# A windowed attention on one Trainium2 core: how the token products are formed, which engine normalises, and when statistics are taken

## The reference, cut to what matters

```python
disp = (x @ w_disp + b_disp).reshape(Bx, Tx, NH, BD).transpose(0, 2, 1, 3)
val = (x @ w_val + b_val).reshape(Bx, Tx, NH, HS).transpose(0, 2, 1, 3)
disp_win = _windows(disp, delta)                       # 32 tokens back
strain = disp_win - disp[:, :, :, None, :]
strain_for_state = strain @ w_state + b_state
state = (strain_for_state * cmask_f[None, None, :, :, None]).sum(axis=3) / valid_counts[None, None, :, None]
state_win = _windows(state, delta)
bond_act = gelu(strain @ w_strain + b_strain + state[:, :, :, None, :] @ w_state_i + state_win @ w_state_j + rel_emb @ w_pos)
bond_logits = (bond_act @ w_bond_out)[..., 0] + b_bond_out[0]
damage_act = gelu(strain @ w_damage + b_damage)
damage = jax.nn.sigmoid((damage_act @ w_damage_out)[..., 0] + b_damage_out[0])
logits = bond_logits - damage * 10.0
weights = jax.nn.softmax(jnp.where(cmask[None, None], logits, -jnp.inf), axis=-1)
out = jnp.einsum('bntd,bntde->bnte', weights, val_win)
```

## Time and profile before

| | us |
|---|---|
| median of 3 runs | 3185.65 |
| lowest and highest | 3184.71 and 3186.94 |
| the profiled execution | 3191.0 |
| its span, first to last instruction | 3189.3 |

### The profile page before, as it was taken

How to read it: one execution, slowest core, us unless ns; L and a number is a source line. 1 busy time by engine, 2 the same in 40 slices (tenths; PEclk the granted TensorE clock), 3 DMA queues, 4 the chain that set the end, 5 groups by cost and what they waited for, 6 DMA issues and landing times. The chain is left out here.

```text
span 3189.3 us, 54032 instructions
## 1 busy us (share of the span) xinstructions
PE 2881.4 (90%) x19465; PEld 2047.0 (64%) x19465; DVE 1665.2 (52%) x4524; ACT 1528.2 (48%) x2579; POOL 1339.6 (42%) x1331
## 2 busy tenths in 40 slices
PE   4899999767899999668999997999879999988999
PEld 4799999722344333257999996666546666655666
DVE  4411111168888888554111111566676666655666
ACT  1133333247988888611333332333247777772333
POOL 3544444358999999435444443000043444320000
PEclk9899999978999999868999998999989999999999
DMA  8199999800544444861999997100052333301000
GB/s 281 41 299 327 324 321 327 243 14 14 63 60 59 60 60 60 81 209 41 302 326 323 327 325 240 29 0 0 15 139 71 75 94 98 85 2 37 13 13 20
DMA packets 359983, 431.82 MB, mean 135 GB/s; under 512 B 86449, under 2 KB 314694, under 8 KB 356678
## 3 DMA queue, kind: packets, MB, share of 16 engines
q1 hardware_dynamic: 335174, 395.17, 44.5%
q0 software_dynamic: 24576, 33.57, 5.0%
HBM read 355.80 MB, written 72.88 MB: 134 GB/s over the span
## 5 line engine op out<-in xcount | busy, mean ns | idle before, releaser
L1675 ACT ACTIVATE f_h_t<-f_h_ps,f_b_t 128x128 f32<-128x128 f32 x1024 | 319.4, 363 | 601.2 <-PE f_h_ps L1633 596.2
L2069 POOL TENSOR_TENSOR a_dmg_buf<-a_c 128x2048 f32<-128x2048 f32 x128 | 520.1, 4090 | 63.8 <-PE a_dmg_ps L2117 34.0
L1633 PEld LDWEIGHTS f_h_ps<-f_rows_t,f_w 128*128 128x128 f32 x4096 | 482.7, 194 | 9.9 <-issue 3.5
L1633 PE MATMUL f_h_ps<-f_rows_t,f_w 128*128 128x128 f32 x4096 | 483.9, 277 | 2.3 <-DVE f_rows_t L1687 1.2
L1647 PE MATMUL f_y_ps<-f_w,f_h_t 128*128 128x256 f32 x2048 | 483.5, 379 | 0.0
L1593 POOL DMA_INDIRECT acc_rows<-f_y,f_give x128 | 205.0, 1602 | 491.5 <-DMA acc_rows<-f_y,f_give 460.3
L1647 PEld LDWEIGHTS f_y_ps<-f_w,f_h_t 128*128 128x128 f32 x2048 | 369.9, 190 | 39.9
L1687 DVE COPY f_rows_t<-f_t_ps 128x256 f32<-128x256 f32 x128 | 54.3, 425 | 602.3 <-PE f_t_ps L1621 597.6
L2434 DVE SCALAR_TENSOR_TENSOR a_bond_buf<-a_a,a_small_rep,a_q_ps 128x512 f32<-128x512 f32 x512 | 346.6, 740 | 7.4 <-PE a_q_ps L2234 5.1
L428 DVE SCALAR_TENSOR_TENSOR x_resid<-f_y_ps,f_gate,x_resid 128x256 f32 x512 | 218.9, 479 | 163.6 <-PE f_y_ps L311 158.0
L885 ACT ACTIVATE a_prob<-a_prob,a_neg_top 128x384 f32<-128x384 f32 (+3 forms) x512 | 276.6, 570 | 47.1 <-POOL a_neg_top L702 46.9
(11 more groups left out here) (353 smaller groups left out, 4174.6 us busy)
## 6 DMA issues: line engine op xcount, KB each, us to landing
f_w<-in_L_ffn_w_dram SPq DMA_DIRECT2D x256, 1024.0 KB
a_skewed<-skew SPq DMA_DIRECT2D x32, 512.0 KB, 6.8
a_k_s<-parts SPq DMA_DIRECT2D x16, 768.0 KB, 7.9
acc_rows<-x_resid SPq DMA_DIRECT2D x17, 512.0 KB, 5.3
xn_rows<-f_xn SPq DMA_DIRECT2D x16, 512.0 KB, 3.0
x_resid<-acc_rows SPq DMA_DIRECT2D x16, 512.0 KB, 7.4
a_vals<-val_rows SPq DMA_DIRECT2D x64, 128.0 KB, 3.8
skew<-a_bond SPq DMA_DIRECT2D x128, 64.0 KB, 10.2
```

Of the source, the lines that this page charges most:

```text
L1633: last = nc.tensor.matmul(h_ps[n // HB][:, (n % HB) * P:(n % HB + 1) * P], w1_sb[s][:, c, n * P:(n + 1) * P], rows_t[e % 2][:, c, :], star ...
L1675: nc.scalar.activation(h_t[k][:, n, :], h_ps[n // HB][:, (n % HB) * P:(n % HB + 1) * P], ACT.Gelu, bias=b1_t[:, n, e:e + 1]).then_inc(gelu ...
L2069: nc.gpsimd.tensor_tensor(dmg_buf[n % RING][:, :, :], places(c_sb[h], first_place(dg)), c_sb[h][:, PAD:].unsqueeze(1).broadcast_to([P, DG, ...
```

## The change

1. disp itself is made (DISP, two passes: xn transposed times w_disp, with b_disp added by VectorE's copy), then transposed (DT, two passes), and the means are those of disp. a, c and q are products of `disp_t` and the means with the five block-diagonal 128 x 128 matrices of `inner`: two products each for a and q, one for c. `token_w` and its making at the entry go away. The bank has NTP = 12 passes a batch; the steps of all passes are set anew, and the first values pair is in step 3 instead of 7.
2. ScalarE normalises (Identity with scale 1/std and bias −mean/std, two instructions each in steps 2 and 3) instead of GpSimd. VectorE makes `less_mean` = −mean/std.
3. In the softmax, GpSimd's subtraction goes from step 3 to 4 (after one more damage chunk), the exponentials from 5 to 6 and the sums from 7 to 8; after the last batch they keep their old places.
4. The statistics of batches 1 to 7, their square root and the split of the output bias are at the entry, between the passes of batch 0.

The core of the diff (lines that are only "..." mark what is left out):

```diff
-    NTP = 8
-    XN, XM, A0, C0, A1, C1 = 0, 2, 4, 5, 6, 7
-    A1_Q, C1_Q, Q1_Q = 0, 3, 4
-    V_Q = (7, 15)
-    XN_Q, XM_Q, A0_Q, C0_Q, Q0_Q = 6, 8, 10, 12, 13
+    NTP = 12
+    XN, DISP, DT, XM, A0, C0, A1, C1 = 0, 2, 4, 6, 8, 9, 10, 11
+
+    A1_Q, C1_Q, Q1_Q = 0, 1, 2
+    V_Q = (3, 15)
+    XN_Q, DISP_Q, DT_Q, XM_Q, A0_Q, C0_Q, Q0_Q = 4, 6, 8, 10, 12, 13, 14
+
+    NORM_Q = 2
+
+    TOP_Q, LESS_Q, EXP_Q, SUM_Q = 3, 4, 6, 8
...
         def softmax_batch(s, q):
+
             i, now = divmod(s, STEPS)
+            if i == B and q > TOP_Q:
+                q -= 1
             return i - 1 if now == q and 0 < i <= B else None
...
-            load(b_disp_sb[:, :], b_disp.rearrange("(h p) -> p h", p=P), allow_slow_non_contiguous=True)
+            load(b_disp_r[:, :], b_disp.partition_broadcast(P))
...
-                if q == 4 and i + 1 < B:
-                    normalise(i + 1)
...
+            def make_disp(i, pair):
+                pe.wait_ge(tok_copied, i * NTP + DISP + pair)
+                if i == 0 and pair == 0:
+                    pe.wait_ge(disp_loaded, 16)
+                for j in range(2):
+                    at = PAD + (2 * pair + j) * P
+                    for c in range(DC):
+                        last = nc.tensor.matmul(tok_ps[:, j * D:(j + 1) * D], xn_t[i % NX][:, c, at:at + P],
+                                                w_disp_sb[:, c, :], start=c == 0, stop=c == DC - 1)
+                last.then_inc(tok_ready, 1)
+
+            def turn_disp(i, h):
+                pe.wait_ge(tok_copied, i * NTP + DT + h)
                 for j in range(TPB):
...
+                    last = nc.tensor.transpose(tok_ps[:, j * P:(j + 1) * P], disp[:, j, h * P:(h + 1) * P], core.ident[:, :])
+                last.then_inc(tok_ready, 1)
...
+            def make_q(i, h):
                 if i:
                     pe.wait_ge(bond_pre, (i - 1) * STEPS + (h + 1) * NQ)
...
+                pe.wait_ge(tok_copied, i * NTP + XM + HALF)
+                nc.tensor.matmul(q_ps[h][:, :], flat(inner[:, TO_Q, :, :]), disp_t[:, h, :], start=True, stop=False)
+                nc.tensor.matmul(q_ps[h][:, :], flat(inner[:, TO_Q_MEAN, :, :]), xm_t[:, h, :],
+                                 start=False, stop=True).then_inc(q_ready, 1)
...
+            def normalise(i, tiles):
+                act.wait_ge(rstd_ready, min(i, 1) + 1)
+                if i:
+                    act.wait_ge(tok_ready, (i - 1) * NTP + XN + DC)
+                for j in tiles:
+                    n = i * TPB + j
+                    last = nc.scalar.activation(xn[:, j, :], core.tile(i + 1, j), ACT.Identity,
+                                                bias=less_mean[:, n:n + 1], scale=rstd[:, n:n + 1])
+                if TPB - 1 in tiles:
+                    last.then_inc(xn_ready, 1)
...
-                if s == 3:
-                    act.wait_ge(var_ready, 2)
-                    nc.scalar.activation(std[:, TPB:], std[:, TPB:], ACT.Sqrt).then_inc(std_ready, 1)
...
+                if q in (NORM_Q, NORM_Q + 1) and i + 1 < B:
+                    normalise(i + 1, (2 * (q - NORM_Q), 2 * (q - NORM_Q) + 1))
...
             def inverse_std(first, end, count):
                 dve.wait_ge(std_ready, count)
...
+                nc.vector.reciprocal(rstd[:, tiles], std[:, tiles])
+                nc.vector.drain()
+                nc.vector.scalar_tensor_tensor(out=less_mean[:, tiles], in0=mean_var[:, tiles, 0], scalar=-1.0,
+                                               in1=rstd[:, tiles], op0=ALU.mult, op1=ALU.mult).then_inc(rstd_ready, 1)
...
+            bn_stats(1, 3)
+            copy_disp(0, 0)
+            bn_stats(3, 4)
+            copy_disp(0, 1)
...
             for h in range(HALF):
...
+                copy_disp_t(0, h)
+            split_bias()
+            copy_means(0, 0)
+            bn_stats(4, 5)
+            copy_means(0, 1)
...
             nc.vector.drain().then_inc(biases_ready, 1)
+            bn_stats(5, B)
+            aggregate(1, B)
             copy_a(0, 0)
+            variances(1, B)
             copy_c(0, 0)
+            inverse_std(1, B, 2)
             dve.wait_ge(pads_ready, 1)
             bond_chunk(0)
```

More of the change, by code:

```diff
@@ L2093, in _ @@
                     damage_chunk(s + 1)
[L2094 removed]
+                j = softmax_batch(s, LESS_Q)
                 if j is not None:
                     less_top(j)
[L2097 to L2098 removed]
         @block.tensor
@@ new lines, in turn_disp, with turn_means @@
+            def turn_disp(i, h):
+                pe.wait_ge(tok_copied, i * NTP + DT + h)
+                for j in range(TPB):
+                    last = nc.tensor.transpose(tok_ps[:, j * P:(j + 1) * P], disp[:, j, h * P:(h + 1) * P], core.ident[:, :])
+                last.then_inc(tok_ready, 1)
+            def turn_means(i, h):
+                pe.wait_ge(tok_copied, i * NTP + XM + h)
+                for j in range(TPB):
+                    last = nc.tensor.matmul(tok_ps[:, j * P:(j + 1) * P], disp[:, j, h * P:(h + 1) * P],
@@ L2238, in begin_a @@
-            def begin_a(i, h):
-                pe.wait_ge(tok_copied, i * NTP + (A0, A1)[h])
-                for c in range(DC):
-                    nc.tensor.matmul(tok_ps[:, :], token_w[:, c, h, TO_A, :], xn_t[i % NX][:, c, PAD:],
-                                     start=c == 0, stop=False)
-            def end_a(i, h):
-                for c in range(DC):
-                    last = nc.tensor.matmul(tok_ps[:, :], token_w[:, c, h, TO_A_MEAN, :], xm_t[:, c, :],
-                                            start=False, stop=c == DC - 1)
-                last.then_inc(tok_ready, 1)
+                pe.wait_ge(tok_copied, i * NTP + XM + HALF)
@@ L2291, in _ @@
+                nc.tensor.matmul(tok_ps[:, :], flat(inner[:, TO_C, :, :]), disp_t[:, h, :],
+                                 start=True, stop=True).then_inc(tok_ready, 1)
             pe.wait_ge(small_ready, 1)
@@ L2564, in bn_stats, with aggregate @@
                         nc.vector.bn_stats(stats[:, i * TPB + j, :], core.tile(i + 1, j))
-            def variances(first, end):
+            def aggregate(first, end):
                 nc.vector.drain()
@@ L2569, in variances @@
                     nc.vector.bn_aggr(mean_var[:, t, :], stats[:, t, :])
+            def variances(first, end):
                 nc.vector.drain()
@@ L2575, in inverse_std @@
                 dve.wait_ge(std_ready, count)
-                nc.vector.reciprocal(rstd[:, first * TPB:end * TPB], std[:, first * TPB:end * TPB]).then_inc(rstd_ready, 1)
+                tiles = slice(first * TPB, end * TPB)
+                nc.vector.reciprocal(rstd[:, tiles], std[:, tiles])
+                nc.vector.drain()
+                nc.vector.scalar_tensor_tensor(out=less_mean[:, tiles], in0=mean_var[:, tiles, 0], scalar=-1.0,
+                                               in1=rstd[:, tiles], op0=ALU.mult, op1=ALU.mult).then_inc(rstd_ready, 1)
             bn_stats(0, 1)
+            aggregate(0, 1)
             variances(0, 1)
             nc.vector.tensor_copy(select[:, :, :], core.ident[0:BD, 0:BD].unsqueeze(1).broadcast_to([BD, HH, BD]))
-            dve.wait_ge(std_ready, 1)
-            nc.vector.reciprocal(rstd[:, 0:TPB], std[:, 0:TPB])
-            nc.vector.drain()
-            for j in range(TPB):
-                last = nc.vector.tensor_scalar(xn[:, j, :], core.tile(1, j), mean_var[:, j, 0:1], rstd[:, j:j + 1],
-                                               ALU.subtract, ALU.mult)
-            last.then_inc(xn_ready, 1)
+            inverse_std(0, 1, 1)
             dve.wait_ge(rel_loaded, REL_LOADED)
```

247 lines of the change are left out of this document (94 added, 153 removed).

## The result

The changed kernel takes 3168.28 us (median of 6 runs, 3150.57 to 3171.87), the kernel before beside it 3186.3 (6 runs, 3184.71 to 3188.63): a ratio of 0.9936, 95% interval 0.9922 to 0.9951. It is 18 us faster where 43.9 had been forecast. A second thing stands in these numbers: the runs of the changed kernel lie 21 us apart here, those of the kernel before 4. (When both were run again, the two spreads were 20 and 22 us, so the difference did not repeat.)

What follows compares the result with a forecast made beforehand. The limit was taken to change by quarter: TensorE in first and last, nobody in the second, GpSimd in the third. Gains 16.5 + 1.7 + 22 + 3.7 = 43.9 off 3185.65 gave 3141.8 us, range 3120 to 3172.

Steps and rivals of the forecast that it cites:

- batch 0: First batch of the phase: two ScalarE waits, 5.56 and 12.85 us, close; 64.6 us instead of 87.65, 23.0 less.
- entry, first GELU later by: Before the loop: added statistics and split cost 2.7 us, `less_mean` waiting for GpSimd's chunk 3.8; first GELU 6.5 later.
- batch 1: Second batch: pays 2.0 us for ScalarE's normalising, saves waits of 2.81 and 0.88; gains 1.7.
- five steady batches: Batches 2 to 6: each falls to 75.9 us, a gain of 4.4; 22 together.
- batch 7: Last batch: no normalising to pay for, saves the 2.81 and 0.88 us waits whole; gains 3.7.
- rival D: Identity isn't in the GELU table: four loads of 1.28 us in each of seven batches, 36 us; 3178 us; chance 3%.
- The second quarter: Second four steps of a steady batch: ScalarE's 21.0 us busy stays, waits of 2.81 and 0.88 go; 21.0 instead of 24.75.
- VectorE's in the third: Third four steps of a steady batch: VectorE's 18.5 us of work less a lead won earlier gives 17.9 instead of 18.69.
- rival C: Twelve passes chain through bank `tok_ps`, each waiting for VectorE's copy: a batch 8.7 us slower, 3230; decides from 6.8; chance 8%.
- the entry's paragraph: Entry account, closing that after this reciprocal no VectorE instruction of the loop reads SBUF alone; batch 0 with entry 16.5 us less.
- The step that failed: Softmax weights' stores: exponentials one step later cost nothing, since they have until step 13, seven steps later.
- rival A: Only the holes close: steady batch stays at 80.3 us, only 16.5 of batch 0 and 3.7 of batch 7 remain; 3165; chance 18%.

Runs made afterwards that it cites:

- the other two edits: Changed kernel with weights loaded between the stores and `less_mean` ahead of c's copy, here together with the earlier row sums: 3134.94 us, again 3137.61, ratio 0.9825 both times.
- the second trace: The changed kernel run again without edit, on another chip: median 3176.1 us, ratio 0.9918; its profiled execution 3175.3.
- the entry alone: Kernel before with only the statistics of batches 1 to 7, their square root and the output bias split moved to the entry: 3183.16 us, ratio 0.9953.

## Why the prediction was right and wrong

By its own terms, against the profiled execution of after:

| term | forecast | measured |
| --- | --- | --- |
| batch 0 | 23.0 | 23.4 |
| entry, first GELU later by | 6.5 | 8.2 |
| batch 1 | 1.7 | 1.6 |
| five steady batches | 22 | 14.9 |
| batch 7 | 3.7 | 3.8 |
| phase | 43.9 | 35.3 |
| the median of the runs | 43.9 | 18 |

**Right.** The holes of batch 0 closed to 64.29 us (64.6 forecast), without a wait of ScalarE. Identity needed no table load between GELUs, as the rows of step 2 show, so rival D is out; the four activations advance ScalarE by 2 × (4.77 − 3.79) = 1.96 us (2.0). The rule of the Trainium skill, page "ScalarE: Activation LUTs", section "Table sets: the hidden batching unit", that identity is in every set, agrees with these rows. The estimate of 585 ns by section "What ACT_TABLE_LOAD costs" of the same page of the Trainium skill agrees with the 589 ns of the group. The second quarter is 20.86 (21.0). `less_mean` took 4.38 us (3.8 of waiting forecast), until 679.63, where GpSimd's first chunk ends at 679.59 in the trace, and 0.19 when it came ahead of that chunk. By the rule of the Trainium skill, page "SBUF — State Buffer", section "Who interferes with whom", a VectorE instruction with two SBUF inputs contends with a GpSimd instruction that reads SBUF; the trace agrees, and the experiment that moved it shows that it could be avoided. Batch 1's 1.6 us (1.7 forecast) are in part luck: its second quarter won 3.1 and its third 0.9, and the fourth lost 0.5, with the wait for the weights in it.

**Sizes.** The entry came 8.2 us later instead of 6.5, inside its bounds. Of the steady batch's 4.4 us, 3.0 came: in batch 4 the first two quarters are 18.65 and 20.86 as forecast, the third is 18.62 instead of 17.9, the fourth stayed at 19.13 instead of 18.2. The term that failed is VectorE's in the third: I took the row sums as work that its lead would absorb (18.5 less a lead). VectorE is busy for only 14.61 of the 18.62, so its amount of work sets nothing; it is the place of the row sums in the order that counts, behind a wait of 3.06 us for TensorE. With them ahead of it, and the other two edits, the five steady batches average 75.4 and 76.0; that 75.9 had been forecast is in part luck, since it is the third quarter that fell below its forecast (16.2 to 17.4 for 17.9) while the fourth stayed above (18.4 to 20.7 for 18.2). In that fourth quarter TensorE is busy for 18.51 us and waits most of the rest for a copy of the means. So rival C, the chain through the one token bank, is real in part: TensorE waits for copies out of it for 5.0 to 6.6 us a steady batch (up to 7.0 in the second trace, 0.5 to 1.2 before), about the 6.8 from which it would decide. But 2.2 us of that lie in the second quarter, which ScalarE fills, and cost nothing; in batch 4 the 2.36 and 0.95 us of the last two quarters are what is left. One reading of the entry's paragraph was wrong, without an effect on the sum: VectorE does read SBUF alone in the loop, in the row sums and their reciprocal.

**The step that failed.** "The exponentials one step later cost their stores nothing: they have until step 13, seven steps later." I counted steps and didn't price the way: sixteen stores issued in 17 to 23 us in the two traces of after, then four loads which land after a median of 7.2 and 8.8. Where TensorE waited for them in the loop of these traces, the weights came 28.1 to 34.8 us after the exponentials' end; in batch 1, where nothing else holds the loop, TensorE wants them after 26.6 (the run with the loads between the stores, in which it doesn't wait). In the kernel before it had 31.1 us and more. Every gain between step 6 and step 13 shortens that time further, so my other terms worked against this one. Between the two traces of after the waits alone differ by 11 us in the loop and 2 in the tail, and the phase by 21, nearly all of it in the batches with such a wait and in the tail. Not all of that is the wait's: 1.9 us are in step 11 of batch 2, ahead of it. The account closes roughly: the terms above are 8.6 us short of the forecast, and the loads between the stores gave back 0.4 to 0.6%, 12 to 18 us, of the other 17. The median happens to lie at the 3165 of rival A, but not for its reason: the steady batch did not stay at 80.3.

The sign, the range and most terms held; the likeliest value was wrong by the transfer that was put at nothing, and by a smaller part in the steady batch. How often that transfer is waited for can't be said from two traces of the changed kernel; both have such a wait.

**Open.** In many batches of every variant step 11 or 12 lasts 1 to 4 us longer than in others of the same run. VectorE's division starts late, in part of them put down to a releaser that the trace names only as remote. From the run with the loads between the stores, batch 6:

```profile
1187.26 0.42 DVE L2476 TENSOR_TENSOR a_ctx<-a_o_ps,a_inv_sum 128x256 f32<-128x256 f32 x1 [3.30 <-remote]
```

TensorE's sums for it had ended at 1185.01 by their modelled ends. In another part it is TensorE that stands idle without a named releaser: in batch 2 of nine of the eleven traces with the new token products it stops behind the fourth of the same eight products, at the same instruction each time, for 1.0 to 4.2 us (the row of 4.18 above). In each of the nine a packet of the queue that the page calls `instruction` had taken 2.4 to 3.1 us shortly before, where most take 0.9; whether late instructions are the cause no run shows. It isn't all new with the change: with the entry alone step 11 of batch 3 lasts 9.6 us for 5.4 to 7.7 in the other steady batches. The weights are moved through DRAM at that time (a DMA share of 1.1 in the third quarter), but no run took the transfers away, so that they are the cause isn't shown.

## What to carry to other kernels

A round trip through DRAM has a budget: the time from its producer to its consumer. Before moving the producer later, or speeding up what lies between, price the way in full (issue of all stores, landing of the loads) from the rows and compare; and let a piece be loaded as soon as its own stores are out. The profiled execution may be the luckiest one: here it was the fastest of six, 18 us below their median, with 1.7 us of waits in its loop where a second trace had 13.1, so take a second trace before explaining a median by the first. An engine's slack must be read against the pace after the change: GpSimd looked relieved by 5 us of 80, and giving them back cost 32 us over seven batches, 4.6 each, because ScalarE's step of 3.79 is shorter than GpSimd's of 4.02.

## What the runs showed of the hardware

The same sixteen stores of 64 KB occupied the sync queue in batch 1 for 17.3, 18.0 and 20.4 us in three executions (before, after, and after on another chip), and over the whole span the loads behind them landed after a median of 6.8, 7.2 and 8.8 us.

After a wait of TensorE the price isn't over. Windows behind the 2.36 us wait of after, and behind the 6.02 us wait of its second execution (the clock is the number ahead of the last two):

```profile
1022.97:1026.40 3.43, 3.43 (x18) 0.62 (x17) 3.43 (x6) 3.17 (x3) 0.72 (x1) 0.53 0.78 53
```

```profile
811.80:814.00 2.20, 2.19 (x9) 2.10 (x10) 0.19 (x1) 0.19 (x1) 0.00 (x0) 0.50 0.89 280
814.00:818.00 4.00, 4.00 (x18) 0.59 (x16) 4.00 (x7) 4.00 (x3) 0.00 (x0) 0.56 0.86 206
```

TensorE is busy throughout each at a granted clock of 0.50 to 0.56, at or near the level of 1.2 GHz, where it had 1.00 up to the 2.36 us wait: the two groups of products took 1.76 and 1.95 us for 1.06, the transposes 1.11 and 1.06 for 0.66 and 0.60. Behind the 1.50 us wait of the first trace the transposes took 0.66 and 0.60, as elsewhere. My sum counted waits as their own length only.
